# Last mixture of 32 experts as eight lists of four, with one-hots sent along and masks and biases made by products

## The reference, cut to what matters

```python
def _L3_ffn_ref(x, router_w, router_b, W1, b1, W2, b2):
    xf = x.reshape(-1, D)                       # 8192 x 128
    logits = xf @ router_w.T + router_b         # 8192 x 32
    idx = jnp.argmax(logits, axis=-1)
    w1t = jnp.take(W1, idx, axis=0)             # E x 128 x 32
    h = jnp.einsum('nd,ndh->nh', xf, w1t) + jnp.take(b1, idx, axis=0)
    h = jax.nn.relu(h)
    w2t = jnp.take(W2, idx, axis=0)             # E x 32 x 128
    out = jnp.einsum('nh,nhd->nd', h, w2t) + jnp.take(b2, idx, axis=0)
    return jax.nn.relu(out).reshape(x.shape)
...
x = x + _L3_gnn_ref(_layernorm(x), adj, L3_gnn_weight, L3_gnn_bias)
x = x + _L3_ffn_ref(_layernorm(x), ...)
```

## Time and profile before

| | us |
|---|---|
| median of 3 runs | 1954.38 |
| lowest, highest | 1948.59, 1958.46 |
| span of the profiled execution | 1867.1 |
| median less span | 87.3 |
| TensorE busy in the span | 1627.8 (87%) |
| VectorE, ScalarE, POOL busy | 1095.9, 998.9, 786.7 |
| last block, from its first instruction | 1494 to 1867 |
| tile loop, from the first tile's landing | 1721 to 1867 |

### The profile page before, as it was taken

How to read it: one execution, slowest core, us unless ns; L and a number is a source line. 1 busy time by engine, 2 the same in 40 slices (tenths; PEclk the granted TensorE clock), 3 DMA queues, 4 the chain that set the end, 5 groups by cost and what they waited for, 6 DMA issues and landing times. The chain is left out here.

```text
span 1867.1 us, 43356 instructions
## 1 busy us (share of the span) xinstructions
PE 1627.8 (87%) x13366; PEld 1314.2 (70%) x13366; DVE 1095.9 (59%) x4199; ACT 998.9 (53%) x3116; POOL 786.7 (42%) x1358
## 2 busy tenths in 40 slices
PE   7978899988859987999998888879999888884995
PEld 5756677767759985788887566679999845553542
DVE  7933433348737777699998755523333377763552
ACT  5854444446636656666665433246666534441663
POOL 6710000014426666111111677745565434554675
PEclk9989999999969999899999799989999989995998
DMA  3200000010014420000000511122222253105331
GB/s 114 84 1 1 1 1 1 1 27 1 1 36 134 123 80 1 2 3 2 2 3 3 156 47 48 62 62 70 72 71 72 56 150 86 58 24 88 100 86 35
DMA packets 125926, 91.76 MB, mean 49 GB/s; under 512 B 23591, under 2 KB 116554, under 8 KB 125701
## 3 DMA queue, kind: packets, MB, share of 16 engines
q1 hardware_dynamic: 109110, 61.89, 12.6%
q0 software_dynamic: 13568, 25.90, 4.3%
q10 hardware_dynamic: 3024, 1.21, 0.4%
HBM read 57.71 MB, written 33.30 MB: 49 GB/s over the span
## 5 line engine op out<-in xcount | busy, mean ns | idle before, releaser
L1361 ACT ACTIVATE FEAT<-BANKS,FEAT 128x128 f32<-128x128 f32 x544 | 155.5, 368 | 82.1 <-PE BANKS L1314 82.1
L1206 POOL DMA_INDIRECT scratch_made<-FEAT x136 | 144.9, 1065 | 122.6 <-DVE FEAT L1500 119.8
L1061 ACT ACTIVATE EXP<-BANKS,NEGMAX 128x128 f32<-128x128 f32 x512 | 139.4, 383 | 59.5 <-DVE NEGMAX L1073 59.5
L440 ACT ACTIVATE gates<-BANKS,EXP 128x64 f32<-128x64 f32 x384 | 97.4, 314 | 112.6 <-PE BANKS L417 112.6
L1314 PE MATMUL BANKS<-FEAT 128*128 128x128 f32 x1088 | 145.5, 277 | 0.0
L1323 PE MATMUL BANKS<-AUX,FEAT 128*128 x1088 | 144.5, 276 | 0.4 <-ACT FEAT L1361 0.4
L417 PEld LDWEIGHTS BANKS<-AUX,EXP 128*128 128x128 f32 x768 | 95.4, 191 | 69.7 <-DVE AUX L464 69.6
L1198 POOL DMA_INDIRECT scratch_sent<-FEAT,POS x128 | 125.1, 977 | 38.3 <-issue 37.5
L990 POOL COPY EXP<-AUX 128x32 f32<-128x32 f32 x256 | 42.5, 211 | 217.8 <-PE BANKS L1036 217.8
L1314 PEld LDWEIGHTS BANKS<-FEAT 128*128 128x128 f32 x1088 | 133.9, 194 | 0.0
L1323 PEld LDWEIGHTS BANKS<-AUX,FEAT 128*128 128x128 f32 x1088 | 133.2, 193 | 0.6 <-issue 0.6
(11 more groups left out here) (367 smaller groups left out, 4196.0 us busy)
## 6 DMA issues: line engine op xcount, KB each, us to landing
EXP<-in_L_ffn_W SPq DMA_DIRECT2D x128, 128.0 KB, 2.1
FEAT<-scratch_sent SPq DMA_DIRECT2D x136, 64.5 KB
EXP<-scratch_made SPq DMA_DIRECT2D x32, 256.0 KB, 3.4
FEAT<-scratch_sent SPq DMA_DIRECT2D x96, 65.5 KB, 1.9
X<-in_x SPq DMA_DIRECT2D x16, 256.0 KB, 2.9
STAGE<-in_adj SPq DMA_DIRECT2D x16, 256.0 KB, 3.3
scratch_sent<-NONE SPq DMA_DIRECT2D x48, 65.5 KB, 3.3
scratch_sent<-FEAT,POS POOLq DMA_INDIRECT x192, 2.3
```

What stands on the lines that cost most here:

```text
L440: act.activation(gates[:, at, sp_, :], PS[2 * at + par][:, u * B:(u + 1) * B], f, bias=wr["b" + gate]).then_inc(done, 1)
L1061: last = act.activation(tile(EXS[:, par], 4 * k + n), tile(PS[j], c), ACT.Exp, bias=NEGMAX[:, par, 4 * k + n:4 * k + n + 1])
L1206: pool.indirect_dma_start(out=made2, out_offset=bass.IndirectOffsetOnAxis(ap=XI_I[:, t % R_IN, H:ROW2], axis=0), in_=YO[:, t % R_OUT, :], ...
L1361: last = act.activation(tile(HR[:, t % R_H], c), tile(PS[2 + t % 2], c), ACT.Gelu, bias=BT[:, c, t:t + 1])
```

## The change

Four experts share a list. A row of the list carries, ahead of x, a one-hot of four floats that says which expert of the list it is (`AT_X = 4`, rows of 135 floats). The list number (index >> 2) takes the place of the expert in `HOT`, `CAR3`, `rank`, `place` and the tile table: 8 lists, NT3 = 64 + 8 = 72 tiles, 18 quads. Only 8 blanks are written at the start and 8 behind the lists, four on each queue.

A tile is multiplied by the W1 of all four experts at once (128 x 128) and by their W2, stacked to 128 x 128. What belongs to the three other experts is taken out by the first product's bias: the table `BT3` holds, in rows 32j + e, NEVER = -2^100 in the 32 columns of the other experts, b1 in those of expert e, and b2 of it. `norm` gathers the one-hots of four tiles in `OP3`, TensorE turns them to `OT3`, and `mask` multiplies them by the quad's `BR3` over all 128 rows, starting the sums of both banks: four products of 128 columns for the hidden units and one of 512 for the output. The ReLU then makes zeros of the other experts' units. The tile loop goes by quads on all engines; the tile-wise products with 32 rows or columns, and `keep_warm` in this loop, are gone. POOL clears the tables in turns 2 to 4 of the routing loop, and SP loads the weights per list and the biases in 20 small DMAs.

```diff
+NEVER = -2.0 ** 100
...
+        L3, M3 = E3 // 4, 4
...
-        ROW3 = H + 3
+        AT_X, AT_R = M3, M3 + H
+        ROW3 = AT_R + 3
...
-        NT3 = B * T // P + E3
+        NT3 = B * T // P + L3
         NQ = NT3 // 4
...
+                def clear(i):
+                    if i == 0:
+                        pool.memset(BT3, NEVER).then_inc(s.none, 1)
+                        pool.memset(OP3, 0.0).then_inc(s.none, 1)
+                    if i < 3:
+                        pool.memset(BR3[i], 0.0).then_inc(s.none, 1)
+                in_turn(NG, [(0, dev), (2, dev2), (2, clear), (6, send)])
...
+                    if i >= 1 and i < 1 + L3:
+                        k = i - 1
+                        sp.dma_start(sent3[L3 * CAP3 + k * P:L3 * CAP3 + (k + 1) * P, :], NONE3[:, L3 + k:L3 + k + ROW3]
+                                     ).then_inc(s.blank, 16)
+                    if i >= 9 and i < 9 + 4:
+                        sp.wait_ge(s.none, 1)
+                        j = 32 * (i - 9)
+                        for e in range(M3):
+                            sp.dma_start(BT3_G[j + e:j + e + 1, :, F3 * e:F3 * e + F3],
+                                         a["L3_ffn_b1"].rearrange("(g e) f -> e g f", e=M3)[e:e + 1]).then_inc(load_e3, 16)
+                        sp.dma_start(BT3_G[j:j + M3, :, P:2 * P], a["L3_ffn_b2"].rearrange("(g e) d -> e g d", e=M3)).then_inc(load_e3, 16)
...
-                for e in range(0, E3 // 2):
+                for e in range(0, L3 // 2):
                     r = sp.value_load(ZROW3[0:1, e:e + 1]).with_bounds(min_val=0, max_val=ROWS3 - P)
                     sp.dma_start(sent3[bass.ds(r, P), :], NONE3[:, e:e + ROW3]).then_inc(s.ex3_blank, 16)
...
+                def turn(q):
+                    reused(pe, s.ex3_hot, q, 2)
+                    pe.wait_ge(s.ex3_xn, q + 1)
+                    pe.transpose(OB3[q % 2][:, 0:P], OP3[:, q % 2, :], ident[:])
+                    reused(pe, s.ex3_xT, q, 2)
+                    transpose4(pe, PS[q % 2], XN3[:, q % 2], s.ex3_t_ps)
+
+                def mask(q):
+                    pe.wait_ge(s.ex3_hot, q + 1)
+                    pe.wait_ge(s.ex3_w, 8 * (q + 1))
+                    reused(pe, s.ex3_hT, q, 2)
+                    reused(pe, s.ex3_y, q, 2)
+                    for j in range(4):
+                        pe.matmul(tile(PS[2 + q % 2], j), BR3[q % 3][:, j, 0:P], OT3[:, q % 2, :],
+                                  start=(j == 0), stop=False, skip_group_check=True)
+                    pe.matmul(Y3[q % 2].rearrange("p (k h) -> p k h", k=4), OT3[:, q % 2, :], BR3[q % 3][:, :, P:2 * P],
+                              start=True, stop=False, skip_group_check=True)
+
+                def up(q):
+                    pe.wait_ge(s.ex3_xT, q + 1)
+                    for j in range(4):
+                        last = pe.matmul(tile(PS[2 + q % 2], j), WR3[q % 3][:, 256 * j:256 * j + P], tile(XT3[:, q % 2], j),
+                                         start=False, stop=True, skip_group_check=True)
+                    last.then_inc(s.ex3_h_ps, 1)
+
+                def down(q):
+                    pe.wait_ge(s.ex3_hT, q + 1)
+                    for j in range(4):
+                        last = pe.matmul(tile(Y3[q % 2], j), tile(HT3[:, q % 2], j), WR3[q % 3][:, 256 * j + P:256 * j + 2 * P],
+                                         start=False, stop=True, skip_group_check=True)
+                    last.then_inc(s.ex3_y_ps, 1)
+                in_turn(NQ, [(0, turn), (1, mask), (1, up), (2, down)])
...
+                def first(q):
                     reused(act, s.ex3_y_ps, q, 3)
...
+                    for j in range(4):
+                        e = act.value_load(EOFI3[0:1, 4 * q + j:4 * q + j + 1]).with_bounds(min_val=0, max_val=L3 - 1)
+                        rows = slice(32 * j, 32 * j + M3)
+                        act.copy(BR3[q % 3][rows, j, :], BT3[rows, bass.ds(e * 256, 256)]).then_inc(s.ex3_w, 1)
+                        act.copy(WR3[q % 3][:, 256 * j:256 * j + 256], WT3[:, bass.ds(e * 256, 256)]).then_inc(s.ex3_w, 1)
...
+                in_turn(NQ, [(2, units), (0, first)])
...
+                    v.tensor_scalar(PART3[:, par, 0, :], IDX3[:].bitcast(INT32)[:, par, :, 0], 2, None, ALU.arith_shift_right)
+                    v.tensor_scalar(PART3[:, par, 1, :], IDX3[:].bitcast(INT32)[:, par, :, 0], M3 - 1, None, ALU.bitwise_and
+                                    ).then_inc(s.part, 1)
...
+                def xT(q):
+                    v.wait_ge(s.ex3_t_ps, q + 1)
+                    reused(v, s.ex3_h_ps, q, 2)
+                    v.tensor_copy(OT3[:, q % 2, :], OB3[q % 2][:, 0:P]).then_inc(s.ex3_hot, 1)
+                    v.tensor_copy(XT3[:, q % 2, :], PS[q % 2]).then_inc(s.ex3_xT, 1)
...
+                in_turn(NQ, [(4, result), (2, xT), (0, norm)])
```

More of the change, by code:

```diff
@@ new lines, in program @@
+        OT3 = EXP[:, 2048:2048 + 2 * P].rearrange("p (a n) -> p a n", a=2)
+        OP3 = EXP[:, 3072:3072 + 2 * P].rearrange("p (a n) -> p a n", a=2)
+        WT3 = AUX[:, 0:L3 * 256]
+        BT3 = AUX[:, L3 * 256:2 * L3 * 256]
+        BT3_G = BT3.rearrange("p (g n) -> p g n", g=L3)
+        WR3 = [w[:].rearrange("p a n -> p (a n)") for w in (WA, WB, WF)]
+        BR3 = [AUX[:, 4096 + 1024 * k:5120 + 1024 * k].rearrange("p (k n) -> p k n", k=4) for k in range(3)]
+        LE3, PRP3 = (EXP[:, 4200 + 40 * k:4200 + 40 * k + L3] for k in range(2))
@@ L1645, in later @@
                     if i == 0:
-                        sp.dma_start(b1_3[:], a["L3_ffn_b1"]).then_inc(load_e3, 16)
-                        sp.dma_start(W1_3.rearrange("p (e f) -> p e f", e=E3), a["L3_ffn_W1"].rearrange("e d f -> d e f")
-                                     ).then_inc(load_e3, 16)
                         sp.wait_ge(s.ctab, 3)
[L1650 to L1653, removed]
@@ L1779, in down @@
-                def down(t):
-                    q = t // 4
-                    if t % 4 == 3:
-                        reused(pe, s.ex3_y, q, 1)
-                        pe.wait_ge(s.ex3_hT, q + 1)
-                        pe.wait_ge(s.ex3_w2c, 8 * (q + 1))
-                        for j in range(4):
-                            dst = tile(PS[4 + j], 0)
-                            rows, row = slice(F3 * j, F3 * (j + 1)), slice(F3 * j, F3 * j + 1)
-                            pe.matmul(dst, ones[row, :], B2C3[row, q % 3, :], start=True, stop=False)
-                            last = pe.matmul(dst, HT3[rows, q % 2, :], W2C3[rows, q % 3, :], start=False, stop=True)
-                        last.then_inc(s.ex3_y_ps, 1)
@@ L1792, in _ @@
-                pe.wait_ge(s.ex3_tab, 2)
-                pe.wait_ge(s.ex3_bt, 1)
-                in_turn(NT3, [(0, turn), (0, keep_warm), (1, up), (2, down)])
+                def turn(q):
[14 more added lines that the diff above has]
+                              start=True, stop=False, skip_group_check=True)
@@ L1853, in _ @@
-                act.wait_ge(s.ex3_w2, 2 * 16)
-                in_turn(NT3, [(0, first), (2, units)])
+                act.wait_ge(load_e3, (2 * L3 + 4 * (M3 + 1)) * 16)
+                act.wait_ge(s.ex3_tab, 2)
+                act.wait_ge(s.none, 5)
+                in_turn(NQ, [(2, units), (0, first)])
             @block.vector
@@ L2002, in _, with norm @@
-                v.wait_ge(s.ex3_bt, 1)
-                in_turn(NT3, [(0, norm), (1, xT), (3, result)])
+                def norm(q):
+                    reused(v, s.ex3_t_ps, q, 2)
+                    for j in range(4):
+                        t = 4 * q + j
+                        v.wait_ge(s_in3[t % R3], 16 * (t // R3 + 1))
+                        v.tensor_scalar(tile(XN3[:, q % 2], j), XI3[:, t % R3, AT_X:AT_R], XI3[:, t % R3, AT_R:AT_R + 1],
+                                               XI3[:, t % R3, AT_R + 1:AT_R + 2], ALU.mult, ALU.add)
+                    at = 4 * q % R3
+                    v.tensor_copy(OP3[:, q % 2, :].rearrange("p (k c) -> p k c", k=4)[:, :, 0:M3], XI3[:, at:at + 4, 0:M3]).then_inc(s.ex3_xn, 1)
```

190 lines of the change are left out of this document (71 added, 119 removed), and 8 rows, old and new, of the table s.

## The result

The changed kernel took 1902.51 us (median of five runs, 1885.2 to 1906.66) against 1956.35 us of the kernel before (five runs beside them, 1948.59 to 1958.52): ratio 0.9713, 95% interval 0.9673 to 0.9752, 54 us faster. The forecast was 1921.5 us, 33 faster. Direction right; time and size wrong.

What follows compares the result with a forecast made beforehand. POOL's scatters of results, 1.286 us each, were taken as the bound. Tiles -30.9, gap -0.9 and routing loop -1.1 make -32.9 us: 1954.4 to 1921.5 us, range 1912 to 1926.

Steps and rivals of the forecast that it cites:

- Tile count: Last stage's scatters on POOL: 72 tiles instead of 96 spare 24 scatters of 1.286 us, 30.9 us in all.
- The loop of TensorE and VectorE: Tile loop: a quad takes these two engines 4.8 us (4.5 to 5.6), under POOL's 5.14.
- ScalarE: Tile loop: its copies and `units` take 4.0 us a quad (4.0 to 5.2), so it stays under POOL's 5.14.
- Ring: The 24 load buffers of the tile loop: reuse takes 9.8 us where POOL's rhythm allows 11.6, so it fits.
- Gap: Between routing and tiles: first landing 7.8 us earlier, nearly all spent by the new order; first scatter 0.9 us earlier.
- Routing loop: Routing ahead of the tiles: narrower rank products make it 1.1 us shorter (0 to 2.5).
- each 0.1 counts: Routing loop: VectorE waits for TensorE, so 0.1 us less rank time shortens each of 11 turns, 1.1 us.
- clock rival: Tile loop, two rivals: clock flickers, 1932 to 1948 us, chance 0.07; low clock holds, 1975 us, chance 0.04.
- Absolute time: Whole kernel: new span of 1834.2 us plus an unchanged 87.3 us between span and median time gives 1921.5 us.
- the loop didn't pass POOL: Rival, tile loop: TensorE/VectorE or ScalarE need 5.4 to 5.9 us a quad, more than POOL; 1926 to 1936 us, chance 0.17.
- the tile loop's clock didn't flicker: Rival, tile loop: a fifth to half of the quads run at 1.2 GHz; 1932 to 1948 us, chance 0.07.
- the low clock didn't hold: Rival, tile loop: all 18 quads run at the low clock, 8.1 us each; 1975 us, slower than before, chance 0.04.

Runs made afterwards that it cites:

- the reordered one: Changed kernel with xT ahead of result on VectorE and the bias product behind up on TensorE: 1836.16 us against 1836.67 for the changed kernel on the same chip.

## Why the prediction was wrong, and where it was right

The table counts one execution of each on chip 4 from the stage's first `combine` (us). The one of the changed kernel, at 1830.2 us, is the quickest of its four (the others 1836.4 to 1837.0); on chip 13, at 1838.5 us, the sum is 335.2, that is 31.3 less than before.

| part of the last stage | before | changed | difference | forecast |
|---|---|---|---|---|
| first `combine` to last send | 207.3 | 208.8 | +1.5 | -1.1 |
| last send to first load | 11.0 | 2.9 | -8.1 | together |
| first load to first scatter | 12.8 | 18.5 | +5.8 | -0.9 |
| first to last scatter | 122.1 | 91.2 | -30.9 | -30.9 |
| last scatter to the end | 13.4 | 12.1 | -1.3 | 0 |
| sum | 366.5 | 333.5 | -33.0 | -32.9 |

- **Tile count: right**, to a tenth, and the tile count undone alone gave it back (32.5 us, 1.8 of them in the tail).
- **The loop of TensorE and VectorE: right.** 4.78 us measured for 4.8, by 0.36 under POOL. Both ends of its range (4.5, 5.6) were too far out.
- **ScalarE: right.** Its copies start 0.43 us apart, a tile 0.85, a quad 4.0 with `units`. **Ring: right**, behind its first wait POOL has no idle time beyond the usual 0.30 us ahead of a scatter.
- **Gap: right in its mechanism.** The blanks' 8 us came and were spent again by the deeper start. From last send to first scatter it is -2.3 here, and -1.1 and -1.4 in two other executions (chip 13, and the reordered one); forecast -0.9.
- **Routing loop: wrong in sign.** The step that failed is "each 0.1 counts". The rank is 0.1 shorter, as worked out (1591.50 to 1592.53, against 1600.11 to 1601.23 before), but the turn stays 11.50. The product behind it, `keep_warm`, takes the 0.1 back, 1.04 us until the next one starts where it was 0.95. TensorE before, then in the changed kernel of chip 13 (start of the rank, `keep_warm`, the next product):

```profile
1600.11 0.38 PE L1732 MATMUL BANKS<-HOT,UPPER 128*128 128x128 f32 x2
...
1601.23 1.02 PE L1678 MATMUL BANKS<-ident 128*128 128x512 f32 x2
1602.18 1.12 PE L1700 MATMUL BANKS<-b3row,ones 1*128 1x512 f32 x2
```

```profile
1591.50 0.30 PE L1750 MATMUL BANKS<-HOT,UPPER 128*128 128x32 f32 x2
...
1592.53 1.10 PE L1696 MATMUL BANKS<-ident 128*128 128x512 f32 x2
1593.57 1.12 PE L1718 MATMUL BANKS<-b3row,ones 1*128 1x512 f32 x2
```

From the first to the last row it is 2.07 us in both. And the narrower products, which I had priced at nothing but their length, let the clock fall. I had looked for a clock rival in the tile loop alone.

- **Tail:** not in the sum, 1.3 us better (13.4 to 12.1). With 96 tiles in the new pipeline it is 13.9, so it goes with the tile count; by what, no run shows.
- **Absolute time: wrong.** The step that failed is "The median of the runs, 1954.38, is 87.3 above the span; I keep that distance". It took the 87 us for something around the program that the change can't touch. Time minus span is 1.9 us in the first comparison's own profile of the changed kernel and 2.2 on chip 4. With 2 the same sum gives 1836, and the changed kernel took 1836.7 and 1838.4 on the two chips where the kernel before agrees with the profile. That it comes so near is in part luck: by the table the routing loop was mispriced by 2.6 us, and the gap and the tail gave 2.7 back. A distance of 87 us between a span and the runs' times said that the profile and the times are of two conditions; I should have asked which of them the other times would meet.
- **Size of the first comparison's gain: not explained.** There it is 54 us instead of 31. The changed kernel's profile from there, against the one of chip 4, has 31 us more by the first scatter and 24 more in the tile loop, by the holes. Of the 31, 27 come between 1068 and 1240 us, in code that the change doesn't touch. This profile is of the quickest of the five executions, 17 us under their median, so the usual one there lost more than it shows. A quad costs 6.4 us in it. If the kernel before has holes as dense in its tile loop, six quads less are worth 6 x 6.4 = 38 us rather than 31; that is argued and not shown, and leaves 16 of 54 open. Nor is a cause of the holes shown. That POOL goes on (1765.04 above) while both consumers of TensorE's results stop together suggests that the signals from TensorE, or TensorE itself behind its records, are late; the ends of products in a record are modelled, so the trace can't tell these apart. The Trainium skill (NOTIFIC — the notification-queue block, "7.1 Overflow: three behaviours, one of which stalls the engine") names one way in which the recording of an execution can hold up an engine; no run here shows whether it did.

The rivals: the loop didn't pass POOL; the tile loop's clock didn't flicker where it was undisturbed (1.00 from 1718 to 1794 us on chip 4), and fell to 0.83 in stretches in the first comparison, behind holes (behind 3.77 us of idle time, at 1769.85, the bias product took 1.92 us instead of 1.02); the low clock didn't hold.

## What to carry to other kernels

Before you add anything to a profiled span, compare it with the runs' own times: if they are further apart than the 2 us around it, the profile may be from another condition, and then neither the difference nor the ratio has to carry over: here the ratio was 0.984 and 0.983 on two chips, where 0.983 was forecast, and 0.971 in the first comparison. In a loop that one engine's issue paces, count that engine's instructions first: a quarter fewer tiles made the time from first to last scatter a quarter shorter (122.1 to 91.2 us), and nothing done to the other engines in the loop showed until it moved the first instruction of the pacing one. And making products narrower can cost time: what they did for the clock goes with them.

## What the hardware showed that I had not expected

- The same program takes 1863 to 1871 us on five chips and 1949 to 1959 in the first comparison. The changed kernel's profile from there has waits of 4 to 6 us that no record explains.
- Cutting the rank products from 448 to 112 columns a turn made one dip of the granted clock (0.85 in an 11.5 us stretch) and 1.6 us in one turn; putting the unused columns back cost no time and removed it, while one added product of 256 columns cost its full 0.43 us a turn.
- A product of 512 columns behind the rank takes 0.95 us until the next one starts, and 1.04 behind the narrow rank: the 0.1 us that the narrow products spare is gone one product later.
- Nine or twelve warming products ahead of the tiles put the first turn at full clock (its four transposes take 0.60 us, against 1.06). With nine, TensorE sat idle for 2.6 us ahead of the first turn and 2.3 us behind it, and the second turn ran at the low clock again (1.06). With twelve, and two more behind the first turn, the second took 0.60 too.
